# Block-recurrent scan on one core: the residual as a row-masked PSUM copy, tiles in two buffers by parity

## What is computed

```python
# B = 2, S = 1024, D = 256, H = 16 heads of Dh = 16, micro-batches of MB = 16 tokens
k = rope(x @ Wk.T); v = x @ Wv.T            # x is the layer-normed, modulated input
W0 = eye(Dh)                                # for each batch and head
def step(W, kv):
    kc, vc = kv                             # 16 tokens
    z = kc @ W
    grad = kc.T @ ((z - vc) * inv_n)        # inv_n = 2 / (MB * Dh)
    return (W - grad, z)
# scan over the 64 micro-batches, layer norm over D of all z, @ Wo.T, gated, added to x
```

## Time and profile before

| | us |
|---|---|
| median of 3 runs | 1145.43 (1140.72 to 1148.85) |
| span of the profiled execution | 1147.2 |
| the scan, from the first z of tile 0 to the first z statistics after tile 7 (767.50 to 965.05) | 197.55 |
| PE, DVE, ACT, POOL busy, share of the span | 90%, 64%, 33%, 20% |

### The profile page before, as it was taken

The page is one execution under the profiler, slowest core; times in us unless marked ns, Lnnn a source line. Parts: engine busy times, 40 slices in busy tenths (PEclk is TensorE's granted clock), DMA queues, the critical chain, the costliest instruction groups (busy, mean ns, idle before and its releaser), DMA issues. The chain is left out here.

```text
span 1147.2 us, 16580 instructions
## 1 busy us (share of the span) xinstructions
PE 1036.7 (90%) x5736; PEld 859.6 (75%) x5736; DVE 734.3 (64%) x1657; ACT 379.3 (33%) x731; POOL 225.3 (20%) x284
## 2 busy tenths in 40 slices
PE   6799999999999999999779999878999996999997
PEld 5677778777778777777668888767787875777775
DVE  7655665566566555666549787647788775366465
ACT  4233332333332333333225122134444542322220
POOL 2222221222122122222010100131222224111011
PEclk9999999999999999999999999989999998799999
DMA  9200000000000000000030000020000000000000
GB/s 300 94 1 0 0 0 0 0 0 0 0 0 0 0 0 0 0 0 1 19 123 1 1 1 1 1 93 1 0 0 0 1 2 1 1 15 10 15 14 23
DMA packets 19033, 20.56 MB, mean 18 GB/s; under 512 B 4905, under 2 KB 14898, under 8 KB 18994
## 3 DMA queue, kind: packets, MB, share of 16 engines
q1 hardware_dynamic: 18994, 20.05, 5.4%
HBM read 17.95 MB, written 2.10 MB: 17 GB/s over the span
## 5 line engine op out<-in xcount | busy, mean ns | idle before, releaser
L393 POOL TENSOR_TENSOR rope_sum<-rope_cos,rope_sin 128x512 f32<-128x512 f32 x80 | 113.1, 1414 | 266.6 <-DVE rope_sin L511 266.6
L780 PE MATMUL proj<-wo_sb,attn_out_t 128*128 128x256 f32 x512 | 119.8, 394 | 30.6 <-ACT attn_out_t L416 27.6
L780 PEld LDWEIGHTS proj<-wo_sb,attn_out_t 128*128 128x128 f32 x512 | 99.5, 197 | 48.4 <-ACT attn_out_t L416 30.9
L429 ACT ACTIVATE rope_exp<-rope_sum 128x512 f32<-128x512 f32 x80 | 50.5, 631 | 216.7 <-POOL rope_sum L393 216.5
L729 PE MATMUL num<-v_ones,score_masked 128*128 128x129 f32 x512 | 99.9, 277 | 5.9 <-DVE score_masked L569 5.9
L730 PE MATMUL num<-state,q_t 128*128 128x129 f32 x512 | 99.8, 277 | 0.0
L1751 DVE SCALAR_TENSOR_TENSOR m_acc<-m_expert,gates,m_acc 128x256 f32<-128x256 f32 x128 | 61.9, 484 | 56.7 <-PE m_expert L1830 50.4
L729 PEld LDWEIGHTS num<-v_ones,score_masked 128*128 128x128 f32 x512 | 82.7, 193 | 13.4 <-DVE score_masked L569 8.0
L508 DVE TENSOR_TENSOR rope_cos<-proj,cos_sb 128x512 f32<-128x512 f32 x80 | 55.3, 691 | 57.7 <-PE proj L683 57.7
L1551 PE MATMUL g_ps<-t_u,k_rows 128*128 128x128 f32 x512 | 72.6, 285 | 16.6 <-DVE t_u L1400 16.4
L1551 PEld LDWEIGHTS g_ps<-t_u,k_rows 128*128 128x128 f32 x512 | 63.4, 191 | 30.3 <-DVE t_u L1400 27.8
(11 more groups left out here) (205 smaller groups left out, 2040.4 us busy)
## 6 DMA issues: line engine op xcount, KB each, us to landing
a_stage<-in_wqkv SPq DMA_DIRECT2D x6, 512.0 KB, 5.4
wo_sb<-in_wo SPq DMA_DIRECT2D x1, 2048.0 KB, 9.7
a_stage<-in_wgu SPq DMA_DIRECT2D x4, 512.0 KB, 8.5
out<-x_sb SPq DMA_DIRECT2D x16, 128.0 KB, 1.7
x_sb<-in_x SPq DMA_DIRECT2D x2, 768.0 KB, 11.0
f_wmod<-in_wmod SPq DMA_DIRECT2D x1, 1536.0 KB, 10.1
w_sb<-in_w SPq DMA_DIRECT2D x1, 1280.0 KB
a_wmod<-in_wmod SPq DMA_DIRECT2D x1, 1024.0 KB, 6.2
```

Of the source, the lines that this page charges most:

```text
L393: pool.tensor_tensor(y[:, parity], t1[:, parity], t2[:, parity], ALU.add).then_inc(s["y_done"], 1)
L780: mm = pe.matmul(proj[:, b, 0:D], o_t[:, i, :], wo[:, i, :], start=(i == 0), stop=(i == H - 1))
```

## The change

- z is made with the negated keys (`spread_blocks` gets `scale=-1.0`) and added onto the projected values in PSUM, where v stands already. One PSUM tensor `kv_ps` [P, 2, B, 512] (keys in columns 0 to 255, values in 256 to 511) takes the place of `z_ps` and `proj`, with two buffers by the parity of the tile.
- Link 2 is then `residual` on ScalarE: a copy of the values' half of `kv_ps` with the per-partition scale `rows_of[:, n]`, 128x256, into `u`. Since `u` is row-masked, g takes the unmasked keys `kr`; the 128 `spread` copies are gone. `kr`, `v` and `k_diag` get two buffers.
- `keep_z` (VectorE, at n = 0 of the next tile) gets z back as `v - kv_ps`, in place of the copy on ScalarE.
- The cast of `split` moves to ScalarE (`high`, at n = 0 and 1), the subtraction `low` stays on VectorE (n = 1 for batch 0, n = 2 for batch 1).
- On ScalarE everything else stands behind the residuals of a given n: `keep_v` of batch 0 at n = 3, of batch 1 at n = 6, `spread_blocks` at 7, `drain_out` at 4 and 5.
- Fillers move: `z_norm` to n = 1, `z_aggregate` to 2, `z_centre` to 3, `x_norm` to 4, `x_aggregate` to 6, `x_centre` to 7; on TensorE `out_turn` to slot 8, `out_rows` to slots 10 and 12. `k_turn` stays in slots 13 and 14. In the last tile `e_centre` goes to n = 3, `turn_group` to slot 7, `chunk_high` to n = 1 to 3.
- All 8 tiles are written out; the `k_diag` memset on POOL is made in two parts, the second behind the first two `add_rope`.

```diff
             @block.gpsimd
-                pool.memset(k_diag[:], 0.0).then_inc(zeroed, 1)
+                pool.memset(k_diag[:, 0], 0.0).then_inc(zeroed, 1)
...
+                pool.memset(k_diag[:, 1], 0.0).then_inc(zeroed, 1)
+                for c in range(NC):
+                    if c + 1 == NC:
+                        e_rstd(pool, 0)
+                    if c:
+                        for b in range(B):
                             z_rstd_of(b, c)
+                    if c + 1 < NC:
+                        add_rope(c + 1, 0)
+                        if c + 2 < NC:
+                            for b in range(B):
+                                x_rstd_of(pool, b, c + 3)
+                        add_rope(c + 1, 1)
...
             @block.scalar
-                    act.activation(k_rows[:, b, j], kr[:, b], ACT.Copy, scale=rows_of[:, j:j + 1]
-                                   ).then_inc(k_rows_done, 1)
...
+                def residual(c, n, b):
+                    act.wait_ge(z_full, nth(b, c * NMB + n + 1))
+                    act.activation(u[:, b], kv_ps[:, c % 2, b, D:2 * D], ACT.Copy, scale=rows_of[:, n:n + 1]
+                                   ).then_inc(u_done, 1)
...
+                    for n in range(NMB):
+                        for b in range(B):
+                            residual(c, n, b)
+                        if nxt:
+                            if n < 2:
+                                drain_norm(c + 1, n)
+                                high(c + 1, n)
+                            if n == 3:
+                                keep_v(c + 1, 0)
+                            if n == 6:
+                                keep_v(c + 1, 1)
...
             @block.vector
+                    for n in range(NMB):
+                        for b in range(B):
+                            new_w(b, c * NMB + n + 2)
+                        if prev:
+                            if n == 0:
+                                for b in range(B):
+                                    keep_z(c - 1, b)
+                            if n == 1:
+                                for b in range(B):
+                                    z_norm(c - 1, b)
...
+                            if n == 3:
+                                for b in range(B):
+                                    z_centre(c - 1, b)
+                            if n in (5, 6):
+                                out_rows(c - 1, n - 5)
+                        if nxt:
+                            if n in (1, 2):
+                                low(c + 1, n - 1)
+                            if n == 3:
+                                rope(c + 1, 0)
+                            if n == 5:
+                                rope(c + 1, 1)
+                        if ahead:
...
+                            if n == 6:
                                 dve.wait_ge(x_stat, nth(1, c + 3))
+                                for b in range(B):
+                                    x_aggregate(dve, b)
+                            if n == 7:
+                                for b in range(B):
+                                    dve.wait_ge(xn_turned, nth(b, c + 2))
+                                    x_centre(dve, c + 2, b, c + 3)
...
             @block.tensor
+                            if 4 <= slot < 7:
+                                project(c + 1, 0, slot - 4)
+                            if 8 <= slot < 11:
+                                project(c + 1, 1, slot - 8)
+                            if 13 <= slot < 15:
+                                k_turn(c + 1, slot - 13)
+                        if prev:
+                            if slot == 8:
+                                for b in range(B):
+                                    out_turn(c - 1, b)
+                            if slot in (10, 12):
+                                out_rows(c - 1, (slot - 10) // 2)
...
-                                mm = pe.matmul(z_ps[:, b, k * P:(k + 1) * P], k_diag[:, b, k, n * P:(n + 1) * P],
-                                               w[:, b, k], start=(n == 0 and k == 0), stop=(n == NMB - 1),
+                                mm = pe.matmul(kv_ps[:, c % 2, b, D + k * P:D + (k + 1) * P],
+                                               k_diag[:, c % 2, b, k, n * P:(n + 1) * P], w[:, b, k],
+                                               start=False, stop=(n == NMB - 1), skip_group_check=True)
...
-                                mm = pe.matmul(g_ps[:, b, k * P:(k + 1) * P], k_rows[:, b, n, k * P:(k + 1) * P],
+                                mm = pe.matmul(g_ps[:, b, k * P:(k + 1) * P], kr[:, c % 2, b, k * P:(k + 1) * P],
```

More of the change, by code:

```diff
@@ L1281, in _ @@
                 act.wait_ge(self.small_in, 16 * 5)
                 for b in range(B):
-                    drain_norm(b, 1)
+                    drain_norm(0, b)
+                    high(0, b)
                 act.wait_ge(zeroed, 1)
                 for b in range(B):
[L1286 to L1291, removed]
@@ L1404, in step @@
-                        if n == 4 and ahead:
-                            for b in range(B):
-                                x_aggregate(dve, b)
-                        for b in range(B):
-                            new_w(b, c * NMB + (n + 2))
-                        if n == 0 and prev:
-                            for b in range(B):
-                                z_norm(b, c)
-                        if n == 1 and nxt:
-                            for b in range(B):
-                                split(b, c + 2)
@@ L1415, in step @@
-                        if n == 2 and prev:
-                            for b in range(B):
-                                z_centre(b, c)
-                        if n == 3 and nxt:
-                            rope(c + 1, 0, c + 2)
-                        if n == 3 and ahead:
-                            for b in range(B):
-                                x_norm(dve, c + 2, b)
-                        if n == 5 and nxt:
-                            rope(c + 1, 1, c + 2)
-                        if n == 5 and prev:
-                            out_rows(0, c)
@@ L1427, in step @@
-                        if n == 5 and ahead:
-                            for b in range(B):
-                                x_centre(dve, c + 2, b, c + 3)
-                        if n == 6 and prev:
-                            out_rows(1, c)
+                                for b in range(B):
[3 more added lines that the diff above has]
+                                    z_norm(c - 1, b)
+                            if n == 2:
+                                for b in range(B):
+                                    z_aggregate(c - 1, b)
@@ L1434, in step @@
                             e_norms(dve, 0)
[L1435 removed]
+                        if not nxt and n == 3:
                             e_centre(dve, 0)
@@ L1493, in _, with filler @@
                 for b in range(B):
-                    norm_turn(b, 1)
+                    norm_turn(0, b)
                 for b in range(B):
                     for i in range(3):
-                        project(b, 1, i)
+                        project(0, b, i)
                 for b in range(B):
-                    k_turn(b, 1)
+                    k_turn(0, b)
                 pe.wait_ge(self.small_in, 16 * 5)
-                def step(c, prev, nxt, ahead):
-                    def filler(n, end):
-                        slot = 2 * n + end
+                for c in range(NC):
+                    prev, nxt = c > 0, c + 1 < NC
+                    def filler(slot):
@@ L1516, in filler @@
-                        if prev:
-                            if slot == 7:
-                                for b in range(B):
-                                    if nxt:
-                                        pe.wait_ge(h_done, nth(b, c + 2))
-                                    out_turn(b, c)
-                        if not nxt and slot == 6:
-                            for b in range(B):
-                                pe.wait_ge(v_kept, nth(b, NC))
-                            self.turn_group(pe, 0, proj)
```

274 lines of the change are left out of this document (121 added, 153 removed).

## The result

| | before | after |
|---|---|---|
| median, us | 1146.28 (6 runs, 1140.72 to 1148.85) | 1155.36 (6 runs, 1153.61 to 1158.82) |
| ratio, 95% interval | | 1.0083, 1.0063 to 1.0103 |
| span of the profiled execution, us | 1147.2 | 1151.8 |
| scan phase, its first matmul to the MoE's first | 221.1 | 231.7 |
| MoE phase | 170.6 | 166.9 |

The change makes the kernel 0.8% slower, 9.1 us by the medians: the interval excludes no change, but the size stays within the 1% that a measurement of this kernel can hardly tell from none. The profiled spans differ by only 4.6 us, since in this execution the MoE was 3.7 us shorter and what precedes the scan 2.3 us, neither of which the change touches.

A forecast was written before the change was run, and what follows sets the result against it. No engine is full, so order and latency bound the kernel. Tiles 0 to 6 +7.2, tile 7 -0.3 and +2.3, ahead of tile 0 -1.4, clock +2.4 on 1147.2 give 1157.4, or 1155.5 us on the runs' scale; range 1138 to 1162.

The forecast's parts named there:

- the late keys: Slot 14: batch 1's key addition waits on POOL behind the rstd of x, delaying g(7); 2.29 us in tiles 1 to 5.
- The free chain: Unhindered micro-batch, link 2 as a ScalarE residual of 0.50 us: z to g takes 1.27 us.
- The middle tile: Tiles 1 to 5: start of each z group on TensorE (Z2 to Z7) counted from z(0); tile length 26.02 us.
- keep_v: ScalarE, n = 3: batch 0's value copy waits for rope ahead of residual(4), delaying g(4); costs 0.7 us a tile.
- low behind z_norm: VectorE, n = 1: low queued behind z_norm makes the projection in slot 4 wait, delaying g(2); costs 0.5 us.
- The clock: Slot 14's pause lets TensorE's clock fall to half behind 2 of 6 pauses, 1.2 us each; +2.4 us.
- Tile 7: Last tile: -0.3 us by its new order until z_norm, +2.3 us for centres beside POOL's weight split.
- the slow centre: Tile 7, VectorE: 6 centring operations beside POOL's weight split take 794 ns each, not 407; +2.3 us.
- Ahead of tile 0: Cast before the first projection moves to ScalarE, 0.39 us in place of 1.76 beside POOL's memset; -1.4 us.
- The loop: Writing out the scan's loop over tiles was costed at nothing within what is summed.
- The late addition is hidden: Rival: batch 1's keys are ready by z(7)'s end in slot 14, and the clock stays; 1139.8 us, chance 0.25.
- The clock falls in every tile: Rival: TensorE's clock falls behind all six pauses, 6 x 1.2 us in place of 2.4; 1160.3 us, chance 0.15.

The follow-up runs named there:

- e7_busy_wait: The changed kernel with 8 matmuls that nobody reads in slot 14, ahead of the late key turning, in tiles 0 to 5; 1151.21 us.
- e1_pool_order: The changed kernel with the key addition of batch 1 on POOL ahead of the rstd of x, not behind it; 1138.48 us.
- e5_before_late: The kernel before, loop written out, with the aggregation of x on VectorE moved from n = 4 to 6 and its centring from 5 to 7; 1155.93 us.
- e2_keep_v: The changed kernel with ScalarE's copy of batch 0's values behind the residuals of n = 4, not at n = 3; 1147.77 us.
- e9_low_first: e1_pool_order, e2_keep_v and e3_weights_wait combined, plus low of batch 0 ahead of the statistics of z at n = 1 on VectorE; 1124.36 us.
- e3_weights_wait: The changed kernel with POOL's weight split in the last tile waiting until VectorE has centred the MoE's x; 1151.19 us.
- e11_before_look: The kernel before, unchanged, run once more for its trace; 1144.05 us.
- e6_before_unrolled: The kernel before with only the scan's loop over tiles 1 to 5 written out; 1139.13 us.
- e8_dve_residual: e1_pool_order, e2_keep_v and e3_weights_wait combined, with the residual made by VectorE in place of ScalarE; 1140.48 us.

## Why the prediction was right

The prediction was 1155.5 us; 1155.36 was measured. The mechanism and the size of its main term, the late keys, held. The near agreement of the total is luck: 10.2 us were forecast on top of the kernel before, the scan phase grew by 10.6 in the traces, the whole by 9.1 by the medians, and every term of the sum was off by 1 us or more, with both signs.

| us | forecast | in the traces |
|---|---|---|
| tiles 0 to 6 without falls of the clock (175.66 in e7_busy_wait) | +7.2 | +5.82 |
| falls of the clock in the scan | +2.4 | +5.02 |
| tile 7 | +2.0 | +5.93 |
| ahead of tile 0 | -1.4 | -3.16 |
| tile 7's end to the MoE's first matmul | 0 | -3.06 |
| sum | +10.2 | +10.55 |

- **The free chain.** From z to g 1.27 us was forecast; in the changed kernel z(0) of tile 1 starts at 785.03 and g(0) at 786.31, 1.28. The residual takes 473 ns, not 500. The Trainium skill (ScalarE: Activation LUTs, What ACT_TABLE_LOAD costs) gives 492 ns by its formula, an estimate by that page; the trace is 19 ns under it.
- **The middle tile.** Z2, Z3, Z4, Z5, Z6, Z7 of tile 1 were 5.01, 8.36, 10.84, 14.83, 18.17, 21.16, forecast 5.00, 8.33, 10.81, 14.96, 18.31, 21.23; g(7) 24.67, forecast 24.79; the end 25.80, forecast 26.02. Tile 0 was 22.99 (23.24).
- **The late keys** (2.29 us a tile forecast): e1_pool_order took 2.13 off each of tiles 1 to 5 and 1.79 off tile 0 (1.96 forecast), 12.4 in all for 13.4, and e5_before_late put 2.8 a tile, with the clock's falls, onto the kernel before. Shown.
- **keep_v** (0.7 a tile): 0.74 by e2_keep_v. **low behind z_norm** (0.5): 0.53 by e9_low_first. Both shown.
- **The clock.** 2 falls of 1.2 us were assumed; there were 4 in tiles 0 to 6, of 1.25 us each by e7_busy_wait. The price was right and the number wrong, 2.6 us: the two pauses of the earlier trace rows told that either can happen, not how often.
- **Tile 7.** -0.3 and +2.3 were forecast; it was +5.9. The term that was mis-sized is the slow centre, 2.3 us, where tile 7 gets 7.1 shorter without it (e3_weights_wait), the clock's fall behind it included. The price, 0.79 us a centre, read from the earlier trace rows, is what one takes beside POOL operations of 0.7 us. Beside one of 2.3 us a pair took 4.56 (e3_weights_wait: 0.73 without). What it costs is what is left of the other engine's operation, not a factor: each slow centre ended 0.15 us after the POOL operation that it met, of 0.7 us (810.23 to 811.00 in the kernel before) as of 2.3 us (953.54 to 955.75 in the changed kernel).
- **Ahead of tile 0.** -1.4 was forecast. From the scan's first matmul to z(0) it was 8.8 us in place of 12.0, so -3.2. The cast brought the first projection 1.4 us forward, as read from the earlier trace rows. But against the second trace of the kernel before, in which the clock was up as in the changed kernel, z(0) comes only 0.7 us earlier (9.5 to 8.8); the other 2.4 us are a fall of the clock in one execution of the kernel before (e11_before_look), not an effect of the change.
- **The loop.** Costed at nothing, since tiles 6 and 7 were written out already. This step was wrong: it holds for the tiles (0.2 us a boundary), and misses the end of the block, 2.1 us, which no tile shows (e6_before_unrolled). By medians it is 7.8 us in the kernel before, of which about 4 go with a higher granted clock of unknown cause. The changed kernel has the written-out loop too, so its other parts probably cost more than the 9.1 us; the changed kernel with the loop kept was not run.
- **The rivals.** "The late addition is hidden" gave 1139.8: e1_pool_order, in which it is hidden, measured 1138.48. "The clock falls in every tile" supposed six falls where I took two; there were four, halfway. In e5_before_late there were six.

## What to carry to other kernels

Relief of the busiest engine gives nothing where its work isn't what the next link waits for: follow each wait in a moved step through the queue that it stands in, here an aggregation moved by two micro-batches on VectorE, an rstd on POOL behind it, and behind that a key addition that TensorE needed. Look at what an in-order queue has behind an instruction whose input you make later, and move that ahead of it; this one swap was worth 17 us, some 5 of them by the clock, which is more than the 13 us at most that the move to ScalarE is worth by e8_dve_residual. Compare stretches of the traces, not totals, where the clock of an untouched phase differs between single executions by more than what is looked for.

## What the hardware showed that was not expected

- A VectorE operation with one SBUF tensor and two per-partition scalars that starts while POOL runs a two-tensor operation of 128x256 or more doesn't end before it, but 0.15 us after: a pair took 4.56 us beside two POOL operations of 2.3 us each, 0.73 without. One that had started 0.23 us ahead of POOL's took its usual 403 ns (785.90 in the kernel before). `new_w`, which reads PSUM, took its usual 0.87 a pair (960.89) beside the same POOL work in e3_weights_wait. The Trainium skill (VectorE: DVE Perf Modes, Two Vector instructions with no wait between them) says that a one-tensor operation in a two-port mode reads through the second SBUF read interface, which GpSimd shares; that fits, though a test of the mode itself was not run.
- The first instructions of the block behind the one with the scan's loop came 2.07 us later on POOL than behind the same code written out (2.40 against 0.33 us), in both traces of the kernel with the loop.
- With the same pause of 2.08 us in front of the key turning, TensorE's clock fell to 1.2 GHz behind four (tiles 2 to 5) and stayed at 2.4 GHz behind one (tile 1). A pause of 1.74 us in tile 0 left it up there, and the like one of e5_before_late did not. Eight matmuls in the pause kept it up in all tiles.
